# Delta-rule recurrence on one core: y computed by channel, its bank copied by ScalarE instead of transposed by VectorE

## The chip, the core and the metric

The kernel runs on one core of a Trainium2 chip (trn2). Its engines are TensorE (PE for matmuls, PEld for weight loads), VectorE (DVE), ScalarE (ACT), GpSimd (POOL) and SyncE (SP, which here issues DMAs). Each engine runs its own list of instructions in order and waits on semaphores. The metric is the device time of one launch, in microseconds, lower is better.

## The reference

A block with two halves: a delta-rule attention and a mixture of experts, each behind a modulated layer norm. Only the first half's recurrence is touched by the change. Cut to that:

```python
# B=4 sequences, T=1024 tokens, D=256, H=16 heads of DH=64; q, k, v: projection, causal conv of 4 taps, silu
k = k / jnp.maximum(jnp.linalg.norm(k, axis=-1, keepdims=True), 1e-12)
alpha, beta = jax.nn.sigmoid(h @ Wa.T + ba), jax.nn.sigmoid(h @ Wb.T + bb)      # per token and head
def step(S, xs):                                   # S: 64 x 64 for each sequence and head
    kt, vt, qt, at, bt = xs
    v_old = jnp.einsum('bhij,bhj->bhi', S, kt)
    upd = vt - at[..., None] * v_old
    S = jnp.clip(at * S + bt * upd[..., :, None] * kt[..., None, :], -5.0, 5.0)
    return S, jnp.einsum('bhij,bhj->bhi', S, qt)   # y of this token
y = ys * jax.nn.silu(h @ Wg.T + bg)
x = x + ga * (y @ Wo.T)                            # then the mixture of experts
```

## The kernel before

The recurrence is done in chunks of 64 tokens (`CW`), sixteen to a sequence. Tokens of one chunk are summed by matrix products, and only a 64 x 64 state `S` is carried from chunk to chunk. A **turn** is one pair of heads (`h` = 0, 1) of one pair of sequences (`b2` = 0, 1), so there are 16 turns (`TURNS`). Everything is laid out so that four 64 x 64 products, for the four (h, b2), sit in the four quarters of TensorE's array: the first operand and the moving one stand on 64 partitions (a row group), the output on 64 partitions of PSUM (a column group).

For chunk `c` the chain is: `seed_u` (L1613) and `state_into_u` (L1622) make `U` in PSUM from the state; ScalarE's `keep_u` (L731) copies it to SBUF; `state_sum` (L1633) makes the new part of the state; VectorE's `state` (L1052, L1049 for the first chunk) adds it to the part that ScalarE's `carry_state` (L742) has decayed. Then `seed_u` of the next chunk waits for that state (`s_st`).

The output y of two chunks, a pair `k` (0 to 7), is a sum of two products in one PSUM bank, `y_bank`: `y_of_state` (L1651), S times the decayed q (`qg`), and `y_of_u` (L1661), U times the masked matrix `A`. Two products of different row groups that add into the same PSUM cells are kept apart by the semaphore `s_yq`. After two pairs the bank is full (a quarter `q`, 0 to 3), VectorE's `turn_y` (L1058) transposes it in blocks of 32 from token-by-channel to channel-by-token into `yT`, and SyncE's `store_y` (L622) writes each half of a turn to DRAM with eight DMAs.

The order on every engine is written out by hand in one loop: iteration `it` interleaves, chunk by chunk, the chain of turn `it - 1` (`chain`, `tc`), the preparation of turn `it` (`prep`, `u`), the projection of k of turn `it + 1` (`new_k`, `un`), and the bound on the clipping of turn `it - 2` (`bound`, `tb`). Between the chain's steps TensorE does projections (L1386), transposes (L1507) and products of q and k (L1471). GpSimd's `solve` (L948 and L953, 31 rounds) inverts the triangular matrices of turn `u` from the end of `turn_matrix` (L1119, VectorE, end of an iteration) on; at chunk 13 VectorE's `rows_of_x` (L1183) and `turn_x` (L1177) wait for its last round, and also stand behind `state(tc, 13)` in VectorE's order. From there to the next `turn_matrix` runs the tail of an iteration. In the last chain iteration (`it` = 16) TensorE fills in with products of the gate (L122).

## Time and profile before

| | us |
|---|---|
| median of 3 runs | 1870.27 (1864.04 to 1873.93) |
| span of the profiled execution, first to last instruction | 1869.6 |
| the 15 iterations with a solve, `turn_matrix` of the first to that of the last | 55.5 to 1107.6 |
| chain of the last turn | 1171 to 1229 |
| the stages behind the recurrence | from 1248 |
| busy in the span: PE, DVE, POOL, ACT | 1620.9, 1389.8, 1127.0, 895.2 |

The own time of the profiled execution is not listed beside its span; the span lies 0.7 us under the median and inside the range of the three runs. An engine's busy time is a mean over stages; which engine holds up the recurrence has to be read from one iteration, engine by engine. In a timeline a row is a run of instructions of one line, with the start, the time to the last one's end, and in brackets the idle time of the engine before it. A matmul of fp32 leaves two records, so a group of 4 products reads x8.

### The profile page before, as it was taken

The page shows a single profiled execution, that of the slowest core. Times are in us where ns is not written, and L with a number is a line of the kernel's source. Part 1 is how long each engine was busy: PE and PEld are TensorE (multiplying, and loading weights), DVE is VectorE, ACT ScalarE, POOL GpSimd, SP SyncE. Part 2 cuts the span into 40 slices and gives each one's busy share as a digit, 9 for nine tenths or more (in the row PEclk, how much of TensorE's full clock was granted, in tenths as well). Part 3 has the DMA queues.
Part 4 walks back from the last instruction along what each step waited for, and adds up shares of the span by engine and source line. Part 5 has one row for each costly group of instructions (what it writes and reads, how often), then busy time and mean ns, then how long its engine had stood idle before and what let it go on. Part 6 is the DMA issues. An engine that isn't in the chain of part 4 may idle for free. (4 is left out here: it accounts for less than half of the span.)

```text
span 1869.6 us, 59680 instructions
## 1 busy us (share of the span) xinstructions
PE 1620.9 (87%) x24736; PEld 1142.6 (61%) x24736; DVE 1389.8 (74%) x1892; ACT 895.2 (48%) x1768; POOL 1127.0 (60%) x1362
## 2 busy tenths in 40 slices
PE   7778999999988989999988988835999848999997
PEld 4445666666666656566656666625888836666664
DVE  8777888888898888898898887447787664444443
ACT  5745555555655655655556555313444232222221
POOL 0657768768767767768777768017343103666664
PEclk9989989989999999989999988977999859999998
DMA  5221231231231231231231230246333163455543
GB/s 184 49 53 25 69 91 37 67 93 37 67 92 37 67 93 36 67 93 36 69 92 36 65 75 26 69 144 227 135 128 110 46 230 79 94 93 100 96 91 51
DMA packets 89465, 156.59 MB, mean 84 GB/s; under 512 B 15708, under 2 KB 54116, under 8 KB 88108
## 3 DMA queue, kind: packets, MB, share of 16 engines
q1 hardware_dynamic: 73292, 124.80, 22.6%
q0 software_dynamic: 15904, 27.93, 8.1%
q8 instruction: 202, 3.31, 0.8%
q14 instruction: 67, 0.55, 0.1%
HBM read 112.56 MB, written 40.12 MB: 82 GB/s over the span
## 5 line engine op out<-in xcount | busy, mean ns | idle before, releaser
L1386 PE MATMUL d_ps<-hT,turn_shared 128*128 128x512 f32 x768 | 402.8, 632 | 8.4 <-DVE d_Vp L1171 4.6
L953 POOL TENSOR_TENSOR turn_shared<-turn_shared,d_tmp 128x31 f32<-128x31 f32 (+15 forms) x496 | 289.7, 584 | 38.9
L948 POOL TENSOR_TENSOR d_tmp<-turn_shared 128x31 f32<-128x31 f32 (+15 forms) x496 | 286.4, 577 | 38.9
L1024 DVE SCALAR_TENSOR_TENSOR turn_shared<-d_ps,d_cw,turn_shared 128x1023 f32<-128x1023 f32 (+2 forms) x192 | 245.3, 1278 | 15.0 <-ACT turn_shared L682 12.6
L742 ACT ACTIVATE d_S<-d_S,gamma_chunk 128x64 f32<-128x64 f32 x448 | 130.9, 340 | 184.5 <-DVE d_S L1052 144.6
L2539 POOL DMA_INDIRECT m_xt<-rows_scratch,m_slot_i x71 | 70.2, 989 | 183.3 <-DVE m_slot_i L2632 95.7
L1386 PEld LDWEIGHTS d_ps<-hT,turn_shared 128*128 128x128 f32 x768 | 126.8, 192 | 87.6 <-issue 71.4
L2526 ACT ACTIVATE m_hm<-m_ps,m_b_tile 128x128 f32<-128x128 f32 x284 | 80.9, 368 | 206.3 <-PE m_ps L2706 206.3
L122 PE MATMUL o_po<-wo_split,y_high 128*128 128x256 f32 x512 | 101.7, 302 | 44.8 <-DVE y_low L115 44.8
L2549 POOL DMA_INDIRECT out<-m_yo,m_slot_i x71 | 114.2, 1608 | 41.2 <-issue 20.3
L2696 PE MATMUL m_ps<-m_w,m_xs 128*128 x284 | 136.2, 602 | 1.6 <-DVE m_xs L2641 1.0
L2287 POOL TENSOR_TENSOR y<-y,g_sb 128x512 f32<-128x512 f32 x48 | 78.8, 1676 | 94.7 <-ACT g_sb L2271 94.7
L2717 PE MATMUL m_ps<-m_w,m_hm 128*128 x568 | 134.4, 380 | 1.1 <-DVE m_yo L2658 1.1
L1651 PE MATMUL d_ps<-d_S,d_qg 64*64 64x64 f32 x1920 | 133.1, 241 | 1.1
L1024 DVE SCALAR_TENSOR_TENSOR d_v_made<-d_ps,d_cw,d_v_made 128x1023 f32<-128x1023 f32 (+2 forms) x96 | 122.3, 1274 | 14.0 <-ACT d_v_made L682 12.8
L731 ACT ACTIVATE d_U<-d_ps 128x128 f32<-128x128 f32 x256 | 70.0, 273 | 112.7 <-PE d_ps L1622 109.7
L1052 DVE TENSOR_TENSOR d_S<-d_S,d_ps 128x128 f32<-128x128 f32 x224 | 62.7, 280 | 80.8 <-PE d_ps L1633 70.5
L682 ACT ACTIVATE turn_shared<-d_ps,d_cw 128x1024 f32<-128x1024 f32 x64 | 77.0, 1203 | 94.2 <-PE d_ps L1386 93.5
L122 PEld LDWEIGHTS o_po<-wo_split,y_high 128*128 128x128 f32 x512 | 86.9, 208 | 47.2 <-issue 32.0
L1651 PEld LDWEIGHTS d_ps<-d_S,d_qg 64*64 64x64 f32 x1920 | 97.3, 144 | 26.0 <-issue 20.9
L2717 PEld LDWEIGHTS m_ps<-m_w,m_hm 128*128 128x128 f32 x568 | 102.4, 190 | 12.5 <-issue 1.5
L973 POOL MEMSET turn_shared<- 128x1024 f32 x16 | 15.2, 952 | 148.8 <-DVE turn_shared L1119 148.8
(251 smaller groups left out, 3737.2 us busy)
## 6 DMA issues: line engine op xcount, KB each, us to landing
turn_shared<-steps_scratch SPq DMA_DIRECT2D x64, 256.0 KB, 4.2
d_qg<-gamma_scratch SPq DMA_DIRECT2D x64, 256.0 KB, 5.0
y_scratch<-d_yT SPq DMA_DIRECT2D x256, 64.0 KB, 1.8
d_arow<-ab_scratch SPq DMA_DIRECT2D x128, 128.0 KB, 3.1
y<-y_scratch SPq DMA_DIRECT2D x8, 2048.0 KB, 8.7
m_w<-w_in SPq DMA_DIRECT2D x16, 512.0 KB, 10.0
turn_shared<-x_by_half_in SPq DMA_DIRECT2D x8, 512.0 KB, 6.8
rows_scratch<-gates SPq DMA_DIRECT2D x4, 1024.0 KB, 11.6
```

The costliest lines, as they stand in the source:

```text
L122: ins = nc.tensor.matmul(dst, lhs(a).bitcast(F32R), rhs(b).bitcast(F32R), start=first and n == 0, stop=last and n == 2)
L742: last = nc.scalar.activation(S[:, (c + 1) % SLOTS, b2, :], S[:, c % SLOTS, b2, :], ACT.Identity, scale=gC[:, b2, tc * NCW + c:tc * NCW + ...
L948: nc.gpsimd.tensor_tensor(tv, Tq[:, s + 1:, s].rearrange("p (r a) -> p r a", a=1).broadcast_to([P, left, known]), X[:, s, 0:known].rearran ...
L953: nc.gpsimd.tensor_tensor(X[:, s + 1:, 0:known], X[:, s + 1:, 0:known], tv, ALU.subtract).then_inc(s_sub, 1)
L1024: nc.vector.scalar_tensor_tensor(out=dst[:, j + 1:], in0=src[:, 0:T - 1 - j], scalar=cw[:, u // BP % 2, n, 2 - j:3 - j], in1=dst[:, j + 1: ...
L1386: return nc.tensor.matmul(dst[:, g, :], w[:, m % 2, n, dc, :], hT[:, dc, at:at + G], start=(dc == 0), stop=(dc == DC - 1))
L1651: last = nc.tensor.matmul(y_ps(c, h, b2), qg[rows64(h), tc % 2, b2, here(c)], S[rows64(h), c % SLOTS, b2, :].rearrange("p (j v) -> p j v", ...
L2287: nc.gpsimd.tensor_tensor(y[:, g % 2, m, :], y[:, g % 2, m, :], gate_kept[g][:, m, :] if g < EARLY else g_sb[:, i % 4, :], ALU.mult).then_ ...
L2526: last = nc.scalar.activation(hm[:, j % 2, f * P:(f + 1) * P], ps[:, 2, f * P:(f + 1) * P], ACT.Gelu, bias=b1_t[:, f, j:j + 1])
L2549: nc.gpsimd.indirect_dma_start(out, bass.IndirectOffsetOnAxis(ap=slot_i[:, j:j + 1], axis=0), yo[:, j % YRING, :], None, compute_op=ALU.ad ...
L2696: last = nc.tensor.matmul(ps[:, j % 2, :], xs[:, j % 2, dc * P:(dc + 1) * P], w1_s[:, bass.ds(e, 1), dc, :].rearrange("p a f -> p (a f)"), ...
L2717: last = nc.tensor.matmul(dst, hm[:, j % 2, f * P:(f + 1) * P], w2_s[:, bass.ds(e, 1), f, :].rearrange("p a d -> p (a d)"), start=f == 0, ...
```

## The change

The products of y change places: the state and U are now the first (stationary) operand and q and A the moving one, so that y comes out with the channel on the partition (head `h` in the rows, sequence `b2` in the columns). The bank then needs no transpose: ScalarE copies it as it is (`keep_y`), and VectorE's `turn_y` is gone. The two row groups are now those of `b2` in the products of U, and both add into the same cells, so `y_of_u` is parted in two calls, and the second waits on `s_yq` for the first; `y_of_state`, now with one row group for each column group, is one call where it was two. `store_y` writes with four DMAs, each of 128 partitions with two runs of 512 bytes, where it had eight of 32 partitions with two runs of 1024 bytes.

```diff
         def y_ps(c, h, b2):
-            return y_bank[rows64(b2), :].rearrange("p (h j t) -> p h j t", h=2, j=2)[:, h, :, c % 4 * CH:(c % 4 + 1) * CH]
+            return y_bank[rows64(h), :].rearrange("p (b j c t) -> p b j c t", b=2, j=2, c=4)[:, b2, :, c % 4, :]
...
                 sp.wait_ge(s_ye, 4 * t + 2 * q + 2)
-                for h, b2 in HEADS:
+                for b2 in range(2):
                     for s in range(2):
                         at = s * T // 2 + q * T // 4
-                        sp.dma_start(y_s[2 * (t % BP) + b2, t // BP][rows64(h), at:at + T // 4]
-                                     .rearrange("(j i) t -> i j t", j=2),
-                                     yT[quad(b2, s), h, :].rearrange("p (j t) -> p j t", j=2)).then_inc(s_yo, 16)
+                        sp.dma_start(y_s[2 * (t % BP) + b2, t // BP][:, at:at + T // 4].rearrange("p (q t) -> p q t", q=2),
+                                     yT[:, :, (2 * b2 + s) * P:(2 * b2 + s + 1) * P]).then_inc(s_yo, 16)
...
+            def keep_y(t, q):
+                act.wait_ge(s_y, HC * t + 2 * (q + 1))
+                if q % 2 == 0 and 2 * t + q // 2:
+                    act.wait_ge(s_yo, 64 * (2 * t + q // 2))
+                nc.scalar.activation(yT[:, q % 2, :], y_bank, ACT.Identity).then_inc(s_ye, 1)
...
-            def turn_y(t, q):
-                dve.wait_ge(s_y, HC * t + 2 * (q + 1))
-                if q % 2 == 0 and 2 * t + q // 2:
-                    dve.wait_ge(s_yo, 128 * (2 * t + q // 2))
-                nc.vector.transpose(flat(yT[:]).rearrange("p (a t) -> p a t", t=G // 2)[:, :, q % 2 * P:(q % 2 + 1) * P],
-                                    y_bank.rearrange("p (a t) -> p a t", t=P)).then_inc(s_ye, 1)
...
-            def y_of_state(tc, k, h):
...
+            def y_of_state(tc, k):
...
                 for c in ((1,) if k == 0 else (2 * k, 2 * k + 1)):
                     for b2 in range(2):
-                        last = nc.tensor.matmul(y_ps(c, h, b2), qg[rows64(h), tc % 2, b2, here(c)],
-                                                S[rows64(h), c % SLOTS, b2, :].rearrange("p (j v) -> p j v", j=2),
-                                                start=opens and (c == 1 or c % 2 == 0), stop=False)
+                        for h in range(2):
+                            last = nc.tensor.matmul(y_ps(c, h, b2), S[rows64(h), c % SLOTS, b2, :],
+                                                    qg[rows64(h), tc % 2, b2, here(c)].rearrange("p (j t) -> p j t", j=2),
+                                                    start=k % 2 == 0 and b2 == 0 and (c == 1 or c % 2 == 0), stop=False)
                 last.then_inc(s_yq, 1)
 
-            def y_of_u(tc, k):
-                pe.wait_ge(s_yq, 2 * (HC * tc + k) + 2)
-                pe.wait_ge(s_ue, NCW * tc + 2 * k + 2)
+            def y_of_u(tc, k, b2):
+                if b2 == 0:
+                    pe.wait_ge(s_yq, 2 * (HC * tc + k) + 1)
+                    pe.wait_ge(s_ue, NCW * tc + 2 * k + 2)
+                else:
+                    pe.wait_ge(s_yq, 2 * (HC * tc + k) + 2)
                 for c in (2 * k, 2 * k + 1):
-                    for h, b2 in HEADS:
-                        last = nc.tensor.matmul(y_ps(c, h, b2), A[rows64(b2), tc % 2, h, c, :],
-                                                U[rows64(b2), c % KEPT, h, :].rearrange("p (j v) -> p j v", j=2),
-                                                start=False, stop=c % 4 == 3 and h == 1)
-                last.then_inc(s_y, 1)
+                    for h in range(2):
+                        last = nc.tensor.matmul(y_ps(c, h, b2), U[rows64(b2), c % KEPT, h, :],
+                                                A[rows64(b2), tc % 2, h, c, :].rearrange("p (j t) -> p j t", j=2),
+                                                start=False, stop=c % 4 == 3 and b2 == 1)
+                last.then_inc(s_y if b2 else s_yq, 1)
```

`keep_y` stands in ScalarE's order behind `keep_u` and `carry_state` of chunks 4, 9 and 11 (quarters 0, 1, 2) and of chunk 0 of the next iteration (quarter 3), where `turn_y` stood in VectorE's. On TensorE every `y_of_u(tc, k)` becomes `y_of_u(tc, k, 0)` and `y_of_u(tc, k, 1)` one behind the other, in the old place. The joined `y_of_state` takes these places: for k = 1, 2 and 6 it stands whole between `seed_u` and the next `state_into_u` (chunks 2, 5, 12), where before only one half stood there and the other in chunk 3, 6 or 13; for k = 0 and 4 whole ahead of `seed_u` (chunks 1, 10), before one half on either side of it; for k = 3 whole behind `state_into_u` of chunk 8, before half of it behind the `seed_u` of that chunk; for k = 5 both halves stood together already (chunk 11); for k = 7 whole ahead of `w_product`.

TensorE's order at chunk 11 of the first iteration of the loop, before: the products of the state are L1651, those of U L1661, seeds L1613, `state_into_u` L1622, `state_sum` L1633.

```order
L1651 MATMUL d_ps<-d_S,d_qg 64x2x32 [waits d_state,d_y]
L1651 MATMUL d_ps<-d_S,d_qg 64x2x32 x3
L1651 MATMUL d_ps<-d_S,d_qg 64x2x32 [waits d_y_of_state]
L1651 MATMUL d_ps<-d_S,d_qg 64x2x32 x3
L1613 MATMUL d_ps<-d_Vp,gate_second 64x64 [waits d_state,d_u_kept]
L1613 MATMUL d_ps<-d_Vp,gate_second 64x64 x3
L1661 MATMUL d_ps<-d_U,d_A 64x2x32 [waits d_u_kept,d_y_of_state]
L1661 MATMUL d_ps<-d_U,d_A 64x2x32 x7
```

The same place of the changed kernel, where the lines are L1650, L1663 and L1615:

```order
L1650 MATMUL d_ps<-d_qg,d_S 64x2x32 [waits d_state,d_y]
L1650 MATMUL d_ps<-d_qg,d_S 64x2x32 x7
L1615 MATMUL d_ps<-d_Vp,gate_second 64x64 [waits d_state,d_u_kept]
L1615 MATMUL d_ps<-d_Vp,gate_second 64x64 x3
L1663 MATMUL d_ps<-d_A,d_U 64x2x32 [waits d_u_kept,d_y_of_state]
L1663 MATMUL d_ps<-d_A,d_U 64x2x32 x3
L1663 MATMUL d_ps<-d_A,d_U 64x2x32 [waits d_y_of_state]
L1663 MATMUL d_ps<-d_A,d_U 64x2x32 x3
```

The number of products is the same; the wait on `d_y_of_state` between two halves has moved from the products of the state to those of U.

ScalarE's order at chunks 4 to 5 of the changed kernel; before, the row L802 is not there, and the others follow one another:

```order
L733 ACTIVATE d_U<-d_ps 128x128 [waits d_u]
L744 ACTIVATE d_S<-d_S,gamma_chunk 128x64 [waits d_state]
L744 ACTIVATE d_S<-d_S,gamma_chunk 128x64
L802 ACTIVATE d_yT<-d_ps 128x512 [waits d_y]
L733 ACTIVATE d_U<-d_ps 128x128 [waits d_u]
L788 ACTIVATE d_ktok<-d_ps 128x1024 [waits d_k_turned]
```

The copy of the bank now stands ahead of the next `keep_u` (L733, before L731).

## Rows read from the trace of the kernel before

**Rows 1.** First lines of the page: span, busy time of each engine.

```profile
span 1869.6 us, 59680 instructions
...
PE 1620.9 (87%) x24736; PEld 1142.6 (61%) x24736; DVE 1389.8 (74%) x1892; ACT 895.2 (48%) x1768; POOL 1127.0 (60%) x1362
```

**Rows 2.** Windows: stretch in us, busy of PE, PEld, DVE, ACT, POOL, clock, DMA.

```profile
413.00:458.00 45.00, 43.50 (x741) 27.32 (x741) 39.47 (x52) 25.77 (x54) 39.28 (x66) 1.00 0.20 49
458.00:480.00 22.00, 17.72 (x546) 13.27 (x542) 20.64 (x21) 14.66 (x21) 13.42 (x7) 0.84 0.26 76
1171.20:1229.00 57.80, 53.65 (x791) 38.23 (x792) 27.88 (x51) 21.95 (x59) 3.86 (x2) 0.94 0.19 53
```

**Rows 3.** One line's instructions, L1119: duration ns, first and last start.

```profile
L1119 DVE STREAM_TRANSPOSE turn_shared<-turn_shared x16: 1945/1973/1989, 55.5 to 1107.6; 128x1024 f32<-128x1024 f32 x16
```

**Rows 4.** Timeline of VectorE, one turn: start, us, idle before and its releaser.

```profile
416.29 0.29 DVE L1052 TENSOR_TENSOR d_S<-d_S,d_ps 128x128 f32<-128x128 f32 x1 [0.84 <-PE d_ps L1633]
...
457.82 0.29 DVE L1052 TENSOR_TENSOR d_S<-d_S,d_ps 128x128 f32<-128x128 f32 x1 [1.00 <-PE d_ps L1633]
458.03 2.09 DVE L1183 STREAM_TRANSPOSE turn_shared<-turn_shared 128x1024 f32<-128x1024 f32 x1
...
479.82 1.96 DVE L1119 STREAM_TRANSPOSE turn_shared<-turn_shared 128x1024 f32<-128x1024 f32 x1
```

**Rows 5.** Timeline of GpSimd in the same turn.

```profile
457.76 0.24 POOL L953 TENSOR_TENSOR turn_shared<-turn_shared,d_tmp 128x31 f32<-128x31 f32 x1
```

**Rows 6.** Timeline of all engines near 736 us, four turns later.

```profile
735.67 0.24 POOL L953 TENSOR_TENSOR turn_shared<-turn_shared,d_tmp 128x31 f32<-128x31 f32 x1
...
737.64 2.09 DVE L1183 STREAM_TRANSPOSE turn_shared<-turn_shared 128x1024 f32<-128x1024 f32 x1
```

**Rows 7.** Timeline of TensorE (PE) in the turn of rows 4.

```profile
419.72 0.68 PE L1661 MATMUL d_ps<-d_U,d_A 64*64 64x64 f32 x16
420.45 0.34 PE L1633 MATMUL d_ps<-d_U,gate_second 64*64 64x64 f32 x8
...
424.36 0.38 PE L1613 MATMUL d_ps<-d_Vp,gate_second 64*64 64x64 f32 x5
...
424.88 0.34 PE L1622 MATMUL d_ps<-d_S,d_WT 64*64 64x64 f32 x8
...
430.08 0.68 PE L1661 MATMUL d_ps<-d_U,d_A 64*64 64x64 f32 x16
430.77 0.45 PE L1613 MATMUL d_ps<-d_Vp,gate_second 64*64 64x64 f32 x8
...
435.58 0.45 PE L1651 MATMUL d_ps<-d_S,d_qg 64*64 64x64 f32 x8
436.25 0.34 PE L1633 MATMUL d_ps<-d_U,gate_second 64*64 64x64 f32 x8 [0.22 <-ACT d_U L731]
...
451.24 0.68 PE L1661 MATMUL d_ps<-d_U,d_A 64*64 64x64 f32 x16
451.70 0.34 PE L1633 MATMUL d_ps<-d_U,gate_second 64*64 64x64 f32 x8
451.99 0.85 PE L1651 MATMUL d_ps<-d_S,d_qg 64*64 64x64 f32 x12
...
452.67 0.28 PE L1651 MATMUL d_ps<-d_S,d_qg 64*64 64x64 f32 x4
```

**Rows 8.** Waits over the span: total us, times, longest us.

```profile
ACT d_U L731 <- PE d_ps L1622: 109.7, 136, 3.7
...
PEld d_ps L1651 <- PE d_ps L1651: 3.3, 16, 0.2
```

**Rows 9.** Groups by line: busy us, mean ns, idle before.

```profile
L1058 DVE STREAM_TRANSPOSE d_yT<-d_ps 128x512 f32<-128x512 f32 x64 | 45.6, 713 | 10.5 <-PE d_ps L1661 5.4 <-DMA y_scratch<-d_yT 4.6
...
L2278 ACT ACTIVATE o_rows<-o_pb 128x512 f32<-128x512 f32 x16 | 9.5, 596 | 105.3 <-PE o_pb L2410 105.3
```

**Rows 10.** DMA issues: count, KB each, median us to landing.

```profile
y_scratch<-d_yT SPq DMA_DIRECT2D x256, 64.0 KB, 1.8
```

More of the change, by code:

```diff
@@ L873, in _ @@
                         keep_w(tc, 1)
+                    if bound and c == 0:
+                        keep_y(tb, 3)
                     if prep and c == 1:
@@ L892, in _ @@
                         carry_state(tc, 5)
+                    if chain and c == 4:
+                        keep_y(tc, 0)
                     if prep and c == 5:
@@ L909, in _ @@
                         carry_state(tc, 10)
+                    if chain and c == 9:
+                        keep_y(tc, 1)
                     if new_k and c == 10:
@@ L914, in _ @@
                         carry_state(tc, 12)
+                    if chain and c == 11:
+                        keep_y(tc, 2)
                     if chain and c == 12:
@@ L1292, in _ @@
                         scalars(u)
-                    if bound and c == 0:
-                        turn_y(tb, 3)
                     if prep and c == 1:
@@ L1327, in _ @@
                         bound_max(tb, 0)
-                    if chain and c == 9:
-                        turn_y(tc, 1)
                     if new_k and c == 9:
@@ L1339, in _ @@
                         tap_k(un, 0, 1)
-                    if chain and c == 11:
-                        turn_y(tc, 2)
                     if new_k and c == 12:
@@ L1781, in _ @@
                         proj_v(u, 1, 3)
-                    if chain and c == 6:
-                        y_of_state(tc, 2, 1)
                     if chain and c == 7:
-                        y_of_u(tc, 2)
+                        y_of_u(tc, 2, 0)
+                        y_of_u(tc, 2, 1)
                     if chain and c == 8:
-                        y_of_state(tc, 3, 0)
+                        y_of_state(tc, 3)
                     if new_k and c == 9:
@@ L1792, in _ @@
                     if chain and c == 11:
-                        y_of_u(tc, 4)
+                        y_of_u(tc, 4, 0)
+                        y_of_u(tc, 4, 1)
                     if new_k and c == 12:
                         proj_k(un, 1, 0)
-                    if chain and c == 13:
-                        y_of_state(tc, 6, 1)
                     if new_k and c == 14:
@@ L1841, in _ @@
                         seed_u(tc, 4)
-                        y_of_state(tc, 1, 1)
                     if chain and c == 4:
-                        y_of_u(tc, 1)
+                        y_of_u(tc, 1, 0)
+                        y_of_u(tc, 1, 1)
                         seed_u(tc, 5)
@@ L1866, in _ @@
                         seed_u(tc, 9)
-                        y_of_state(tc, 3, 1)
                     if chain and c == 9:
-                        y_of_u(tc, 3)
+                        y_of_u(tc, 3, 0)
+                        y_of_u(tc, 3, 1)
                         seed_u(tc, 10)
```

59 lines of the change are left out of this document (28 added, 31 removed).

## The prediction

> **What bounds the kernel now.** The page first: PE is busy for 87% of the span, VectorE for 74%, ScalarE for 48% [rows 1]. The change takes work from VectorE and gives it to ScalarE, so the question is which engine holds up an iteration of the recurrence. `turn_matrix` starts from 55.5 to 1107.6 us, fifteen intervals, so an iteration takes 70.1 us [rows 3]. I took the one from 411.1 to 479.8 us, the shortest kind, and cut it at the moment where `rows_of_x` starts, 458.03. In the first stretch, 413 to 458, PE is busy for 43.50 of 45.00 us, VectorE for 39.47, ScalarE for 25.77. In the second, the tail, VectorE is busy for 20.64 of 22.00 us and PE for only 17.72 [rows 2]. So the tail is VectorE's, 21.8 us from `rows_of_x` to the next `turn_matrix` [rows 4]. None of the four transposes of y stands in it: three stand ahead of chunk 13 and one in chunk 0, behind `turn_matrix`.
>
> What sets the start of the tail? Two things, and they meet. GpSimd's last round ends at 457.76 + 0.24 = 458.00 [rows 5], and `rows_of_x` starts at 458.03. But VectorE's own last step ahead of it, `state(13)`, ran from 457.82 to 458.11 and had waited 1.00 us for PE's `state_sum` [rows 4]; also at chunk 1 VectorE waited 0.84 us for PE [rows 4]. So in the first stretch VectorE has room, PE has none, and GpSimd's solve is level with PE. In other iterations, as at 736 us, GpSimd is done at 735.91 and `rows_of_x` starts at 737.64 [rows 6]: there PE's chain is 1.7 us late and GpSimd has room.
>
> That gives the rule for the sum: what VectorE saves ahead of chunk 13 buys little, and what PE's order loses there is added to every iteration, since GpSimd's room in the short iterations is nil and in the long ones is used up already.
>
> **VectorE's part.** The 64 transposes cost 713 ns each, 45.6 us in all, and 10.5 us of waiting ahead of them [rows 9]: 2.85 us busy in each turn. Bounds: 0 (all of it ahead of chunk 13 goes into VectorE's waits for PE, which grow) and 45.6 us (VectorE sets everything). I take 0, because of the 1.00 and 0.84 us of waiting. If PE's cover were gone, these 2.85 us would be the gain of a turn.
>
> **ScalarE's part.** It gets 64 copies of 128x512 from PSUM. The nearest row is a copy of that shape, 596 ns [rows 9], so 38 us in all, 2.4 us for each turn. Behind each copy the next `keep_u` is queued, and PE's `state_sum` waits for that. `keep_u` waited for PE in 136 cases, 109.7 us, so 0.8 us at a time [rows 8]; that is the room that hides a copy of 0.6 us. I take 0, with 2.4 us a turn as the other end. The copy frees the bank about as early as the transpose did, and PE did not wait for the bank before.
>
> **The store.** Eight DMAs, 1.8 us from issue to landing each [rows 10], become four of twice the size. VectorE waited 4.6 us in all for these landings [rows 9]; ScalarE's `keep_y` of chunk 11 would wait instead. Fewer issues on SyncE's queue should make the last one land no later. I take 0, and 4.6 us as its upper bound.
>
> **PE's part: the waits.** The number of products is the same, and so is their pace: eight records of `y_of_state`, which share a row group, take 0.45 us, and sixteen of `y_of_u`, on the diagonal, 0.68 us [rows 7], so from the first start to the last 0.23 and 0.46 us, if the last record takes 0.22. Where a half waits for the other, the price is seen at chunk 11, the one place where both halves of `y_of_state` stood together (the profile counts 16 such waits [rows 8]): from 451.99 to 452.67 + 0.28 = 452.95, so 0.96 us where sixteen records without a wait take 0.68 [rows 7]. A wait costs 0.28 us. After the change there are eight such waits in a turn (one in each `y_of_u`) and that of chunk 11 is gone.
>
> How many are covered? In chunk 2 `y_of_u` starts at 419.72 and `state_sum` at 420.45, 0.73 us later where 0.46 are needed; in chunk 4 `seed_u` starts 0.69 us after it [rows 7]. Such places (k = 0, 1, 2, 3) have 0.23 to 0.27 us of room, because the next group waits for ScalarE or VectorE: 0.05 us is left of each, 0.2 together. The one at k = 6 stands behind `state_sum(13)` and is in the tail. In chunk 11 `state_sum` follows `y_of_u` by 0.46 us (451.24, 451.70): no room, full price, and so for k = 5 and for k = 7 in chunk 0. That is 3 x 0.28 - 0.28 (the wait that is gone) + 0.2 = 0.76 us.
>
> **PE's part: the places.** `state_into_u` waits until `seed_u` has finished: in chunk 2 seeds start at 424.36, and `state_into_u` at 424.88, 0.52 us later, the length of a group of eight (0.45, as at 430.77) and the semaphore [rows 7]. The half of `y_of_state` behind the seed hides in that. A second half doesn't fit, so it adds 0.23 us in chunks 2, 5 and 12. What it leaves gives nothing back: in chunk 6 that half ran at 435.58 in time in which `state_sum`, at 436.25, waited for ScalarE [rows 7]. In chunk 10 the half that hid behind the seed moves ahead of it, again about 0.2 us. Sum 0.9 us. Bounds for this term: 0, if the order of the records fills the gap after all, and 0.9.
>
> **The sum.** 0.76 + 0.9 = 1.66, and I take 1.6 us, since in chunk 6 `keep_u` is held by ScalarE's own work and takes up some of it. Fourteen iterations at 1.6, and 1.3 for the first, which has no k = 7: 23.7 us. In the last chain PE is busy for 53.65 of 57.80 us [rows 2]; seven more waits at 0.28 make 2.0 us, hidden nowhere but in chunk 0: I take 1.5. Together 25.2 us on the span of 1869.6 [rows 1]: 1894.8. The span stands 0.7 us under the median of the runs shown: about 1895 us, 1.3% slower.
>
> The Trainium skill ("TensorE: Matmul & The Clock Gate", section "Single matmul latency") puts the fixed part of a warm matmul's latency at 398 cycles of 2.4 GHz, 166 ns. A wait for one's own product would cost about that, an estimate from that page. This trace has 0.28 us, semaphore and refill included; by the page's figure the eight waits would cost 0.11 us less each, and the kernel would come out near 1890 us.
>
> **Rivals.**
> 1. VectorE sets the iteration, faster. Its place is VectorE's order ahead of chunk 13; each transpose taken away moves `state` and the taps behind it forward. For it: VectorE is busy for 39.47 of 45 us there, and in iterations such as that of 736 us the tail starts late, behind a transpose. Against it: the 1.00 us wait for PE. Full price 45.6 us less, 1825 us; but GpSimd's solve allows only the lateness, 1.7 us in perhaps half of the iterations, about 12 us: 1858 us. It decides if PE's extra waits stay below 0.5 us a turn. Chance 0.16.
> 2. Covered on both sides, no change: PE's waits fall into times in which it waits anyway, as the gaps of 0.2 us at `state_sum` suggest, and the late iterations give back what the short ones lose. 1865 to 1875 us. Chance 0.15.
> 3. ScalarE's copies delay `keep_u` as well: 0.6 us, four times a turn, fully exposed would be 38 us more, 1933 us; at half of it 1914 us. For it: they stand ahead of `keep_u` in the chain. Against it: the 0.8 us of waiting. Chance 0.12.
> 4. The forecast, PE's waits and places alone: 1882 to 1907 us. Chance 0.57.
>
> **How the numbers follow.** A change of 0.5%, 9.4 us, is about what a measurement of this kernel can tell from none. Slower by more than that: cases 3 and 4 but for a small part of case 4 near its lower end, 0.67. Same: case 2 and that part, 0.17. Faster: case 1, 0.16. The likeliest case gives 1895 us. The range, 1862 to 1913 us, leaves out most of case 1 and the upper half of case 3.
>
> **What the profile after would show.** `turn_y` gone and VectorE's busy time down by 45 us; ScalarE's up by 38 us. About 128 waits of the second `y_of_u` for the first, with 0.28 us between the groups beyond the usual pace. An iteration of 71.6 us in place of 70.1, with a tail that is still 21.8 us; `rows_of_x` about 1.6 us behind GpSimd's last round in every iteration, and VectorE's wait for PE ahead of `state(13)` grown from 1.0 to about 2.5 us. `keep_u` must still wait for PE behind a `keep_y`, not the other way round. I would be wrong if `rows_of_x` starts with GpSimd's last round in all iterations (then PE had room that I don't see), if the tail gets shorter, or if ScalarE is what PE waits for in chunks 1, 5, 10 and 12.

## The result: 6.3 us slower, a quarter of what was forecast

| | before | after |
|---|---|---|
| median of 10 runs each, us | 1868.10 (1864.04 to 1873.93) | 1874.35 (1868.66 to 1880.19) |
| ratio, 95% interval | | 1.0035 (1.0019 to 1.0052) |
| span of the profiled execution, us | 1869.6 | 1872.4 |
| `turn_matrix`, first to last | 55.5 to 1107.6 | 55.8 to 1110.0 |
| an undisturbed iteration | 68.72 | 69.61 |

The profiled execution of the changed kernel took 1873.98 us. Its page, first lines:

```profile
span 1872.4 us, 59552 instructions
...
PE 1615.0 (86%) x24736; PEld 1124.6 (60%) x24736; DVE 1354.9 (72%) x1828; ACT 925.0 (49%) x1832; POOL 1127.0 (60%) x1362
```

Against [rows 1]: VectorE's busy time fell by 34.9 us, where 45 were expected, and ScalarE's rose by 29.8, where 38 were. The durations of all VectorE's instructions sum to 40.8 us less (`turn_y` is gone with 45.6, some others take a little longer), and since records of one engine overlap in time, the busy time falls by less than that. Windows of one undisturbed iteration and of the last chain (stretch, busy of PE, PEld, DVE, ACT, POOL, granted clock, DMA share, GB/s):

```profile
830.00:876.00 46.00, 43.91 (x734) 26.99 (x734) 37.88 (x48) 27.65 (x58) 40.09 (x66) 1.00 0.27 71
876.00:898.00 22.00, 17.97 (x548) 13.46 (x546) 20.63 (x21) 14.63 (x21) 12.47 (x7) 0.84 0.23 69
1174.00:1230.00 56.00, 51.16 (x758) 35.29 (x758) 21.10 (x41) 21.95 (x59) 2.84 (x2) 0.94 0.16 50
```

The columns answer to [rows 2]: PE is still the engine without room ahead of the tail, and VectorE is at 37.88 of 46 us. The line of `turn_matrix`, now L1128, answers to [rows 3]:

```profile
L1128 DVE STREAM_TRANSPOSE turn_shared<-turn_shared x16: 1950/1973/1986, 55.8 to 1110.0; 128x1024 f32<-128x1024 f32 x16
```

The intervals sum to 1054.2 us, 2.1 more than before, so 70.28 for 70.14. That small difference hides two large ones. Here is VectorE at both ends of one undisturbed iteration (828.29 to 897.90, so 69.61 us), and behind it GpSimd's last round in it:

```profile
828.29 1.97 DVE L1128 STREAM_TRANSPOSE turn_shared<-turn_shared 128x1024 f32<-128x1024 f32 x1
...
875.88 0.29 DVE L1068 TENSOR_TENSOR d_S<-d_S,d_ps 128x128 f32<-128x128 f32 x1 [1.29 <-PE d_ps L1635]
876.09 2.09 DVE L1192 STREAM_TRANSPOSE turn_shared<-turn_shared 128x1024 f32<-128x1024 f32 x1
...
897.90 1.98 DVE L1128 STREAM_TRANSPOSE turn_shared<-turn_shared 128x1024 f32<-128x1024 f32 x1
```

```profile
874.80 0.24 POOL L969 TENSOR_TENSOR turn_shared<-turn_shared,d_tmp 128x31 f32<-128x31 f32 x1
```

GpSimd is done at 875.04 and `rows_of_x` (L1192) starts at 876.09, 1.05 us late, where it was 0.03 us late in [rows 4, 5]. VectorE's wait for PE ahead of `state(13)` is 1.29 us, where it was 1.00. The tail is 21.8 us, as before. So PE now sets every iteration, as forecast, but by 1.05 us, and an undisturbed iteration got longer by 0.89 us, where the prediction had 1.6. In this profile fewer iterations are disturbed, too. The waits (total us, times, longest):

```profile
DVE d_S L1068 <- PE d_ps L1635: 113.0, 102, 3.6
...
ACT d_U L733 <- PE d_ps L1624: 89.2, 99, 4.2
...
PEld d_ps L1663 <- PE d_ps L1663: 25.7, 128, 0.3
...
ACT d_yT L802 <- PE d_ps L1663: 19.3, 32, 1.6
```

`keep_u` still waits for PE behind the copies; `keep_y` (L802) waited for PE alone, never for a DMA.

### The profile page after: what moved, and what is told of

Same layout as the page of the kernel before. It is cut to its first block and busy times, and to the rows that moved or that the text cites. A ratio compares the mean times of both kernels' runs of the same rounds, so it can differ in the third digit from the quotient of the medians.

```text
span 1872.4 us, 59552 instructions
## 1 busy us (share of the span) xinstructions
PE 1615.0 (86%) x24736; PEld 1124.6 (60%) x24736; DVE 1354.9 (72%) x1828; ACT 925.0 (49%) x1832; POOL 1127.0 (60%) x1362
## 3 DMA queue, kind: packets, MB, share of 16 engines
q1 hardware_dynamic: 87628, 124.79, 21.8%
## 5 line engine op out<-in xcount | busy, mean ns | idle before, releaser
L969 POOL TENSOR_TENSOR turn_shared<-turn_shared,d_tmp 128x31 f32<-128x31 f32 (+15 forms) x496 | 296.5, 598 | 38.9
L964 POOL TENSOR_TENSOR d_tmp<-turn_shared 128x31 f32<-128x31 f32 (+15 forms) x496 | 279.9, 564 | 38.9
L1663 PE MATMUL d_ps<-d_A,d_U 64*64 64x64 f32 x2048 | 113.8, 227 | 8.4 <-issue 0.2
L733 ACT ACTIVATE d_U<-d_ps 128x128 f32<-128x128 f32 x256 | 70.0, 274 | 90.3 <-PE d_ps L1624 89.2
L1473 PE MATMUL d_ps<-turn_shared 64*64 64x64 f32 x4096 | 77.6, 226 | 27.1 <-DVE beta_turned L1100 12.2
## 6 DMA issues: line engine op xcount, KB each, us to landing
rows_scratch<-gates SPq DMA_DIRECT2D x4, 1024.0 KB, 13.1
```

The source lines that it names most:

```text
L964: nc.gpsimd.tensor_tensor(tv, Tq[:, s + 1:, s].rearrange("p (r a) -> p r a", a=1).broadcast_to([P, left, known]), X[:, s, 0:known].rearran ...
L969: nc.gpsimd.tensor_tensor(X[:, s + 1:, 0:known], X[:, s + 1:, 0:known], tv, ALU.subtract).then_inc(s_sub, 1)
L1663: last = nc.tensor.matmul(y_ps(c, h, b2), U[rows64(b2), c % KEPT, h, :], A[rows64(b2), tc % 2, h, c, :].rearrange("p (j t) -> p j t", j=2) ...
```

## The experiments

The differences are against the kernel before, timed beside it on the same chip, by medians. "Undisturbed" is the interval between two `turn_matrix` in an iteration in which TensorE has no stop (what that is comes below): the value that most such iterations of the profile share.

| kernel | median, us | before beside it | difference | ratio to before, 95% | undisturbed iteration |
|---|---|---|---|---|---|
| changed kernel | 1874.35 | 1868.10 | +6.3 | 1.0035 (1.0019 to 1.0052) | 69.61 |
| 6 changed kernel, timed again | 1875.89 | 1868.28 | +7.6 | 1.0034 (1.0020 to 1.0048) | 69.62 |
| 1 old places | 1867.53 | 1867.45 | +0.1 | 1.0010 (0.9994 to 1.0027) | 69.23 |
| 2 VectorE copies | 1878.22 | 1867.45 | +10.8 | 1.0051 (1.0032 to 1.0071) | 69.70 |
| 3 waits, by sequence | 1936.60 | 1867.45 | +69.2 | 1.0385 (1.0360 to 1.0410) | 73.2 |
| 4 halves about the seeds | 1863.26 | 1867.45 | -4.2 | 0.9980 (0.9964 to 0.9995) | 69.21 |
| 7 waits, by head | 1884.26 | 1868.28 | +16.0 | 1.0066 (1.0044 to 1.0087) | 69.66 |
| 8 last pair about the seed | 1861.37 | 1868.28 | -6.9 | 0.9962 (0.9947 to 0.9976) | 69.04 |
| 11 the same, in the changed kernel | 1874.61 | 1870.31 | +4.3 | 1.0021 (1.0003 to 1.0038) | 69.43 |
| 13 before, code moved by 64 | 1872.64 | 1869.19 | +3.5 | 1.0028 (1.0012 to 1.0044) | 68.73 |
| 14 changed, code moved by 64 | 1879.76 | 1869.19 | +10.6 | 1.0059 (1.0038 to 1.0079) | 69.62 |
| 9 before, code moved by 128 | 1868.34 | 1870.31 | -2.0 | 0.9989 (0.9970 to 1.0007) | 68.73 |
| 10 changed, code moved by 128 | 1882.71 | 1870.31 | +12.4 | 1.0074 (1.0045 to 1.0104) | 69.62 |
| 12 kernel 8, code moved by 128 | 1870.16 | 1870.31 | -0.2 | 1.0008 (0.9988 to 1.0028) | 69.05 |
| 15 before, code moved by 192 | 1874.71 | 1869.19 | +5.5 | 1.0037 (1.0019 to 1.0056) | 68.72 |
| 16 changed, code moved by 192 | 1883.06 | 1869.19 | +13.9 | 1.0087 (1.0067 to 1.0106) | 69.62 |
| 17 before, gamma rows late | 1862.39 | 1868.60 | -6.2 | 0.9971 (0.9952 to 0.9990) | 68.73 |
| 18 changed, gamma rows early | 1879.16 | 1868.60 | +10.6 | 1.0058 (1.0035 to 1.0081) | 69.62 |

### The terms of the sum: kernels 1, 2, 4, 8, 11

Kernel 1 takes back the joining of `y_of_state`:

```diff
-            def y_of_state(tc, k):
+            def y_of_state(tc, k, b2):
...
                     if chain and c == 5:
                         seed_u(tc, 6)
-                        y_of_state(tc, 2)
+                        y_of_state(tc, 2, 0)
...
+                    if chain and c == 6:
+                        y_of_state(tc, 2, 1)
```

> The changed kernel with y_of_state parted by sequence and its halves at the old places (no wait between them), so that only the waits inside y_of_u are left of what the change adds to TensorE's order. Theory A (read from the two traces: places worth about 0.55 us of an undisturbed iteration, waits 0.3): iteration of the recurrence 69.6 -> 69.1 us, 8 us less than the changed kernel, about 1866 us. Theory B (the prediction's sizes: places 0.9, waits 0.76, and VectorE's saved time gives 0.8 back): 13 us less, 1861 us. Theory C (places cost nothing, all is waits): as the changed kernel, 1874 us.

Measured: 6 to 7.5 us less than the changed kernel, and 0.38 us of an undisturbed iteration. The prediction's 0.9 us for the places was more than twice the measured price. Chunk by chunk (starts of `state_into_u` and `state_sum` from `turn_matrix` on, changed kernel less before): the place in chunk 2 costs 0.19 us by chunk 3, of which 0.17 come back in chunk 4, where `state_sum` waits for ScalarE less (0.31 us for 0.48); that in chunk 5 costs 0.08, given back in chunk 6; those in chunks 10 and 12 cost 0.24 and 0.18.

Kernel 2 gives the copies to VectorE, at the old places of `turn_y`:

```diff
-                    if chain and c == 4:
-                        keep_y(tc, 0)
...
                     if chain and c == 4:
+                        copy_y(tc, 0)
                         update_max(tc, 0)
```

> The changed kernel, but VectorE copies the bank, at the places where it transposed it before; ScalarE does not. TensorE's order is that of the changed kernel. It tells what relieving VectorE gave. Theory A (VectorE's time ahead of chunk 13 is nearly all waiting for TensorE, and ScalarE's copies cost nothing): 0 to 5 us more than the changed kernel, 1874 to 1879 us. Theory B (the relief gave back 0.8 us of the 1.66 us that TensorE lost in each iteration): 12 us more, 1886 us. Theory D (ScalarE's copies delayed keep_u and cost something themselves): less than the changed kernel.

Measured: 3 to 4.5 us above the changed kernel, 0.09 us of an undisturbed iteration. VectorE's relief was worth about this, and ScalarE's copies cost nothing that taking them away would give back. The kernel does both at once, so the 0.09 us are their sum; but chunk by chunk ahead of the tail no `state_into_u` or `state_sum` starts earlier than in the changed kernel. The prediction's two zeros were right.

Kernel 4 is kernel 1 with the second half of `y_of_u` behind the seed that follows, for k = 1, 3, 6, 7:

```diff
                     if chain and c == 4:
                         y_of_u(tc, 1, 0)
-                        y_of_u(tc, 1, 1)
                         seed_u(tc, 5)
+                        y_of_u(tc, 1, 1)
```

> The version with the old places, and in addition the second half of y_of_u stands behind the seed that follows it (k = 1, 3, 6; for k = 7 the seed of chunk 1 stands between the halves), so that the seed runs in the time of the wait. Theory A: iteration 68.7 to 68.8 us, where GpSimd's rounds set it; 11 to 13 us less than the changed kernel, 1861 to 1863 us, unless TensorE's stops of about 1 us come back (13 us in the trace of before, 3 in that of after). Theory B: 1.7 us less for each iteration than the changed kernel is not to be had, since GpSimd holds the iteration at 68.7: the same 1861. Theory E (moving halves apart costs as much as it hides): as the version with the old places alone.

The iteration got shorter by 0.02 us only (that the time fell by 4.3 us against kernel 1 all the same, no run here explains). For k = 7 the move gives 0.17 us (`state_sum` of chunk 1 starts within 0.01 us of where it did before the change), and for k = 1 it loses 0.19: there the seed waits for the state anyway, and the second half had its place ahead of it. So kernel 8 moves k = 7 alone:

```diff
+                    if bound and c == 0:
+                        y_of_u(tb, 7, 0)
                     if chain and c == 0:
                         seed_u(tc, 1)
                     if bound and c == 0:
-                        y_of_u(tb, 7, 0)
                         y_of_u(tb, 7, 1)
```

> The version with the old places, and only the last pair's second half of y_of_u (k = 7, chunk 0) behind the seed of chunk 1; k = 1, 3, 6 as in the changed kernel. Theory A (the wait in chunk 0 costs 0.2 us, moving k = 1 behind its seed costs 0.23, the rest is one or the other alike): an undisturbed iteration of 68.97 us, where the two versions before had 69.23 and 69.21; 4 us less than the version with the old places, about 1863 us. Theory E (nothing to be had): 1867 us.

69.04 us against 68.97 expected, and 1861.4 us: the parts add up. In the changed kernel itself the same move is worth 0.18 us of an iteration:

> The changed kernel, in which only the order of three calls in chunk 0 differs: first half of y_of_u of the last pair, seed of chunk 1, second half. y_of_state stays at the changed kernel's places. Theory A (the parts add up: this move was worth 0.20 us with the old places): an undisturbed iteration of 69.4 us where the changed kernel has 69.6; 3 us less, about 1872 us. Theory E (what is won in chunk 0 is lost at the places of chunks 2 and 5): 1874 to 1875 us.

### What a wait costs: kernels 3 and 7

Both put a wait between two halves of `y_of_u` into the kernel before, kernel 3 by sequence as in the change, kernel 7 by head:

```diff
-                for c in (2 * k, 2 * k + 1):
-                    for h, b2 in HEADS:
+                for b2 in range(2):
+                    for c in (2 * k, 2 * k + 1):
...
+                    if b2 == 0:
+                        last.then_inc(s_yq, 1)
+                        pe.wait_ge(s_yq, 3 * (HC * tc + k) + 3)
```

> The kernel before, in which y_of_u is parted by sequence and the second half waits for the first, as in the change; all else, with VectorE's transposes and the places of y_of_state, as before. Theory A: 0.3 us for each iteration, 4 to 5 us more than before, about 1873 us. Theory B (the prediction's 0.76 us and the one more at chunk 11 that is not taken away here, 1.04): 11 to 16 us more, 1879 to 1884 us. Theory C (the waits are hidden): as before, 1868 us.

It was 69 us slower, which no theory had. TensorE in kernel 3:

```profile
440.05 0.34 PE L1633 MATMUL d_ps<-d_U,gate_second 64*64 64x64 f32 x8 [0.48 <-ACT d_U L731]
440.19 1.20 PE L1662 MATMUL d_ps<-d_U,d_A 64*64 64x64 f32 x13
```

The first eight records of L1662 started over 0.43 us, where eight records of `y_of_u` in the changed kernel take 0.23. In the layout before, the products of one sequence all stand on one quarter of the array. Over the whole run the median of a half was 0.456 us from first to last start on one quarter, and 0.230 us on two. The experiment had changed the pace as well as the wait, so it says nothing on the wait. Kernel 7 parts by head, which keeps two quarters in turn:

> The kernel before with a wait between the halves of y_of_u, parted by head this time, so that each half still alternates between two quarters of the array (eight records in 0.23 us, where the halves by sequence stood on one quarter and took 0.46). Theory A: waits cost 0.5 us for each iteration (as the version with the old places shows: 69.23 against 68.72 us), 7 us more than before, 1875 us. Theory B (the prediction's 0.28 us for each wait that has no room, 1.04 us with that of chunk 11 kept): 15 us more, 1883 us. Theory H (what the first experiment on waits lost came from the waits, not from the one quarter): 60 us more.

Theory B, the prediction's own price, was right here: 16.0 us where 15 were expected, 0.94 us of an undisturbed iteration where 1.04 were. TensorE at chunk 11 of the kernel before, of kernel 7, and of the changed kernel (two views of it, the second closer):

```profile
870.05 0.34 PE L1622 MATMUL d_ps<-d_S,d_WT 64*64 64x64 f32 x8
870.33 0.68 PE L1661 MATMUL d_ps<-d_U,d_A 64*64 64x64 f32 x16
870.79 0.34 PE L1633 MATMUL d_ps<-d_U,gate_second 64*64 64x64 f32 x8
...
872.52 0.27 PE L1622 MATMUL d_ps<-d_S,d_WT 64*64 64x64 f32 x1
```

```profile
877.00 0.34 PE L1622 MATMUL d_ps<-d_S,d_WT 64*64 64x64 f32 x8
877.28 0.90 PE L1662 MATMUL d_ps<-d_U,d_A 64*64 64x64 f32 x13
877.97 0.27 PE L1633 MATMUL d_ps<-d_U,gate_second 64*64 64x64 f32 x1
...
878.31 0.85 PE L1651 MATMUL d_ps<-d_S,d_qg 64*64 64x64 f32 x12
...
879.34 0.90 PE L1662 MATMUL d_ps<-d_U,d_A 64*64 64x64 f32 x13
880.03 0.27 PE L1622 MATMUL d_ps<-d_S,d_WT 64*64 64x64 f32 x1
```

```profile
868.73 0.34 PE L1624 MATMUL d_ps<-d_S,d_WT 64*64 64x64 f32 x8
868.89 0.79 PE L1663 MATMUL d_ps<-d_A,d_U 64*64 64x64 f32 x11
...
869.88 0.68 PE L1650 MATMUL d_ps<-d_qg,d_S 64*64 64x64 f32 x16
870.42 0.41 PE L1615 MATMUL d_ps<-d_Vp,gate_second 64*64 64x64 f32 x7
...
870.68 0.80 PE L1663 MATMUL d_ps<-d_A,d_U 64*64 64x64 f32 x11
```

```profile
869.47 0.27 PE L1635 MATMUL d_ps<-d_U,gate_second 64*64 64x64 f32 x1
```

From `state_into_u` (L1622, L1624) to `state_sum` (L1633, L1635) kernel 7 takes 0.97 us and the changed kernel 0.74; before it was 0.74 as well ([rows 7] show its second part, 0.46 from `y_of_u` on). The gap itself is alike in both: the second half starts 0.28 us behind the last record of the first (medians over the 128 groups: 0.285 us in kernel 7, 0.278 in the changed kernel). But in kernel 7 and before, `y_of_u` starts 0.28 us behind `state_into_u`, in the changed kernel 0.16, and its first eight records take 0.19 us there for 0.23. What the first half gains so pays for most of the gap. So a wait has the price that the prediction gave it, 0.28 us, but at k = 4 the changed kernel pays nothing for it. From `state_sum` to the next `state_into_u`, with k = 5 between, kernel 7 takes 2.06 us and the changed kernel 1.80, before 1.73: 0.33 us for the wait in the old layout, 0.07 in the changed kernel, where the wait in `y_of_state` is gone as well. Kernel 1, with the new layout and the old places, has 0.78 and 1.88 us here, so it pays 0.04 and 0.15. At k = 7 all three pay the same, 0.18 to 0.19.

### Where the rest went: stops for code

Undisturbed, an iteration is 0.89 us longer, and the last chain 2.4 us (from the first `state` to the last, 50.5 before, 52.9 after). 15 x 0.89 + 2.4 = 15.8 us, but 6.3 and 7.6 were measured. The two traces also differ in something that neither the diff nor the prediction names. TensorE in iteration 4 of the kernel before:

```profile
342.97 1.13 PE L1386 MATMUL d_ps<-hT,turn_shared 128*128 128x512 f32 x2
344.03 0.27 PE L1633 MATMUL d_ps<-d_U,d_ktok 64*64 64x64 f32 x1
345.81 0.34 PE L1633 MATMUL d_ps<-d_U,d_ktok 64*64 64x64 f32 x7 [1.52 <-issue]
```

For 1.52 us it stands in the middle of a group, and the row says "issue": nothing it waits for is late. I count such stops of 0.3 us or more, where no semaphore stands between the products on either side. Ahead of the tail the first profile of before has seven, 8.0 us together, and that of the changed kernel three, 2.4 us. `rows_of_x`, summed over the fifteen iterations, stands 13.3 us further behind GpSimd's last round before and 2.8 us after than it would in undisturbed iterations; that sum holds all lateness, not the stops alone. The thirteen stops of the kernel before that lie between 127 and 1230 us have one thing in common: 1.3 to 1.6 us ahead of each stop's end a 16 KB packet of the DMA queue "instruction" has landed. The reading is that TensorE waits for its own program; the row of a packet doesn't name an engine, and the kernels with moved code test it.

Kernel 5 (kernel before, unchanged, one profile) and kernel 6 (changed kernel, unchanged):

> The kernel before, unchanged, profiled in another execution. In the first profile TensorE stops seven times by 0.8 to 1.5 us between the chunks ahead of the tail, with nothing late that it waits for, 13 us in all. Each of these stops ends 1.2 to 1.5 us after a 16 KB packet of the DMA queue named instruction has landed. Theory F (the stops sit where the blocks of TensorE's code begin, so that they come back): at least five of the seven at the same chunk of the same iteration. Theory G (each execution draws its own): other places, another sum.

> The changed kernel, unchanged, profiled and timed again. Its first profile has three such stops ahead of the tail, 2.4 us in all. Theory F: the same three, at 157, 578 and 928 us. Theory G: others. The time again about 1874 us, 6 us more than before.

Four of seven came back before (5.0 us into iteration 4, 30.5 into 7, 3.4 into 9, 3.5 into 15), with other lengths; this execution took 1859.7 us. (The 13 us in the text above are the lateness of `rows_of_x`, not the sum of the seven stops.) In the changed kernel one of three did (7), and three in the tails. The places recur, the lengths vary, so both theories are half right. The 128 waits that the next kernels add ahead of TensorE's first product move its code and change neither a product nor the order:

```diff
+            for _ in range(128):
+                pe.wait_ge(s_c, 16)
             pe.wait_ge(s_wm, 32)
```

> The kernel before with 128 more semaphore waits, all long met, ahead of TensorE's first product, where it waits for its first loads anyway. No product and no order changes; TensorE's code from there on lies 128 instructions further. Theory F (the stops of 0.3 to 1.5 us, each ending 1.2 to 1.5 us after a 16 KB packet of the instruction queue has landed, sit where a block of TensorE's code ends): in the two profiles of before four stops are at the same chunks (5.0 us into iteration 4, 30.5 into 7, 3.4 into 9, 3.5 into 15), here those places are free of stops and others have them. The sum of the stops may be less or more than 4 to 8 us ahead of the tail, and the time moves by up to 10 us either way. Theory G (the stops come from the work that goes on at those places, whatever the code's position): the same four places, the same time, 1868 us.

> The changed kernel with the same 128 waits ahead of TensorE's first product. Theory F: its stops (65.6 us into iteration 2, 66.4 into 3, 66 into 8, which both profiles have) go elsewhere; the undisturbed iteration stays 69.61 us. If the changed kernel had fewer stops than before by its code's position alone, then with both kernels moved the difference between them is another than 6 to 7 us, up to the 13 us that its longer iteration is worth (0.89 us, fifteen times). Theory G: the same places, 1874 us.

> The fastest version so far (old places, last pair's second half behind the seed, 1861 us) with the same 128 waits ahead of TensorE's first product. Theory F: other places of the stops, the undisturbed iteration of 69.04 us as before; the time within 5 us of 1861. Theory K (its lead of 7 us over the kernel before is owed to the position of its code, since its undisturbed iteration is 0.3 us longer than that of before): the lead is gone or halved against the kernel before that is moved as well.

The old places are free of stops, and others have them (3.0 us into iteration 4, 3.6 into 5, 29.9 into 8, 3.7 into 11, 30.5 into 14 among them). In kernel 10, too, the places of the changed kernel are free and others have stops (30.1 us into iteration 2, 65.8 into 4, 30.2 into 8, 30.3 into 14). Theory F holds. Kernel 12 is the sobering one: the lead of kernel 8 over the kernel before, 6.9 us, is gone once its code lies 128 instructions further: 1870.16 us, 1.8 above kernel 9. And the moved pair differs by 14.4 us. Part of that is ahead of the recurrence: iteration 1 begins at 130.2 us in kernel 10 and at 126.4 in kernel 9. Two more positions:

> The kernel before with 64 semaphore waits, long met, ahead of TensorE's first product. Theory F (position of the code): undisturbed iteration 68.72 us, stops at other places than with 0 and 128 waits; the time anywhere from 1860 to 1876 us. Theory G (position is nothing): 1868 to 1870 us.

> The changed kernel with 64 such waits. Theory L (the order's own price is 0.89 us for each iteration, 13 us, and 6 to 7 us is the lucky position): 11 to 20 us more than the kernel before that is moved alike. Theory M (the pair at 128 is the odd one, the price is 6 us): 3 to 9 us more.

> The kernel before with 192 such waits; the first product starts 1 to 3 us later than unmoved, which is the same in both kernels. Theory F: undisturbed iteration 68.72 us, again other places of the stops, 1862 to 1879 us.

> The changed kernel with 192 such waits. Theory L: 11 to 20 us more than the kernel before that is moved alike. Theory M: 3 to 9 us more. The undisturbed iteration stays 69.61 us by either.

The differences, changed less before, are 6.3 and 7.6 (unmoved, measured twice), 7.1, 14.4 and 8.4 us; the mean over the four positions is 9.2. Theory L expected 11 to 20 and fails at 64 and 192; so luck of position isn't the main thing. Only kernels moved alike are compared here, for the added waits also hold up the start: the first product comes at 8.3 us unmoved and at 8.5, 9.6 and 13.1 us with 64, 128 and 192 waits, the same to 0.1 us in both kernels (for 192, 1 to 3 us later were expected, and it was 4.7), so that much of kernel 15's +5.5 us is not the position. In the profiles the fifteen iterations together exceed fifteen undisturbed ones by 9.4 to 21.3 us in the five of the kernel before (mean 16.4), and by 6.2 to 18.6 us in the five of the changed kernel (mean 11.1). That is 5.3 us less, and 15.8 less 5.3 is 10.5 us, near the 9.2 measured; the spread shows how little one pair of profiles says. What is systematic shows when the stops are sorted by place. Between 3 and 7 us into an iteration the five profiles of the kernel before (unmoved twice, then 64, 128 and 192) have 4, 3, 1, 4 and 3 stops, 2.4 to 5.3 us in a profile; the five of the changed kernel have none. (One of the four at 128, 0.41 us, stands at a met semaphore; it ends 1.5 us behind a packet of code like the rest.)

### The wait that moved: kernels 17 and 18

Why there? The gamma rows, four transfers of 256 KB into `qg` for the next turn, are issued by SyncE. It waits in `gamma_rows` for `s_yq`, which before the change was complete with `y_of_state` of the last pair, in the tail. The change counts the first half of `y_of_u` on the same semaphore, and for the last pair that half stands in chunk 0 of the next iteration. SyncE's issues, the kernel before and the changed one, iteration 4 (`turn_matrix` at 339.3 and 337.6):

```profile
336.70 2.37 SPq L615 DMA_DIRECT2D d_qg<-gamma_scratch  x4
```

```profile
341.00 2.37 SPq L615 DMA_DIRECT2D d_qg<-gamma_scratch  x4
```

They went from 2.6 us ahead of `turn_matrix` to 3.4 us behind it. And this is what they had been in the way of (queue, kind: packets, MB, share of 16 engines), first in the kernel before from 336 to 343 and from 343 to 345 us, then in the changed kernel from 336 to 340:

```profile
q1 hardware_dynamic: 728, 1.64, 86.1%
```

```profile
q1 hardware_dynamic: 89, 0.07, 16.7%
q8 instruction: 1, 0.02, 3.5%
```

```profile
q1 hardware_dynamic: 257, 0.31, 21.5%
q8 instruction: 1, 0.02, 1.5%
```

Before, data takes 86% of the DMA engines for seven microseconds, and the window lists no packet of code; one is loaded at 343.4, and TensorE goes on 2.4 us later. In the changed kernel the packet comes at 338.4, 0.8 us into the iteration. This is no single case: over the fifteen iterations the first packet of code behind `turn_matrix` starts at a median of 3.8 us in the kernel before and at 1.4 in the changed one. The last two kernels swap this one wait and nothing else:

```diff
-                    sp.wait_ge(s_yq, 2 * HC * (u - 1))
+                    sp.wait_ge(s_y, HC * (u - 1))
```

in the kernel before (kernel 17, gamma rows late), and in the changed one (kernel 18, gamma rows early)

```diff
-                    sp.wait_ge(s_yq, 2 * HC * (u - 1))
+                    sp.wait_ge(s_yq, 2 * HC * (u - 1) - 1)
```

> The kernel before, in which the load of the gamma rows waits for y_of_u of the last pair where it waited for y_of_state of it. Nothing else changes. Theory N (these four transfers hold up the block of code that TensorE needs in chunks 0 and 1, and the changed kernel has them out of the way by accident): the loads are issued 3 to 4 us behind turn_matrix, the block of code is loaded 1 to 2 us behind it, the stops between 3 and 7 us are gone, and the time is 4 to 8 us less than before, 1860 to 1864 us. Theory O (the load's place is nothing): 1868 us.

> The changed kernel, in which the load of the gamma rows waits for y_of_state of the last pair alone, as it did before the change. Theory N: the loads are issued 3 us ahead of turn_matrix, stops of 0.4 to 1.5 us come back between 3 and 7 us of three or four iterations, and the time is 4 to 8 us more than the changed kernel, 1879 to 1883 us, 11 to 15 more than before. Theory O: 1875 us.

Both moved the way theory N said: kernel 17 to 6.2 us less than before (ratio 0.9971, 0.9952 to 0.9990), kernel 18 to 3.0 to 4.3 us more than the changed kernel had over before, a little under the 4 to 8 of the theory. The first is clear of its interval; the second is not by itself, as the intervals of kernel 18 and of the changed kernel overlap, but the packets and the stops in its trace moved as the theory says: the median start of the first packet is 1.6 us in kernel 17 and 3.5 in kernel 18. The whole of its fifteen iterations shows no loss, though: they exceed undisturbed ones by 7.6 us, in the changed kernel by 10.0 and 11.4. So in the new order the 3 to 4 us rest on the medians alone. SyncE and TensorE in iteration 4 of kernel 17 (`turn_matrix` at 333.3), where the group that was cut is whole:

```profile
336.97 3.30 SPq L615 DMA_DIRECT2D d_qg<-gamma_scratch  x4
```

```profile
342.67 0.35 PE L1633 MATMUL d_ps<-d_U,d_ktok 64*64 64x64 f32 x8
```

and of kernel 18 (`turn_matrix` at 335.4), where it is cut again:

```profile
332.81 2.37 SPq L615 DMA_DIRECT2D d_qg<-gamma_scratch  x4
```

```profile
340.40 0.27 PE L1635 MATMUL d_ps<-d_U,d_ktok 64*64 64x64 f32 x1
341.64 0.34 PE L1635 MATMUL d_ps<-d_U,d_ktok 64*64 64x64 f32 x7 [0.98 <-issue]
```

Between 3 and 7 us kernel 17 has no stop and kernel 18 has three, in iterations 4, 10 and 15.

So the order of TensorE costs 10.6 us with the gamma rows early in both (kernel 18 against before), and 12 to 14 with them late in both (+6.3 or +7.6 for the changed kernel, less the -6.2 of kernel 17). The moved load gives back 3 to 6 of it, surely in the old order and likely in the new. Two other engines wait for the same semaphore, ScalarE's `carry_state` and VectorE's `state` of chunk 0; in the changed kernel's profile these waits come to one of 0.8 us.

## Why the prediction was wrong, by its own steps

1. **What bounds the kernel.** Right. PE's chain ahead of chunk 13 sets the start of the tail, the tail kept its 21.8 us, and a loss of PE is added to every iteration. The late chain that it saw at 736 us [rows 6] stood in iteration 9, one of those with stops for code.
2. **VectorE's part, 0.** Right: 0.09 us of an undisturbed iteration, 3 to 4.5 us in all (kernel 2), of a bound of 45.6.
3. **ScalarE's part and the store, 0.** Right. `keep_u` waited for PE 89.2 us in all where it had waited 109.7 [rows 8]: the copies went into that room. The four larger stores took 3.1 us from issue to landing where the eight had taken 1.8, but nothing waited for them.
4. **PE's waits, 0.76 us.** The price of one, 0.28 us, held; kernel 7 bore out the whole step within 0.1 us in the layout in which it was measured. The smaller price, by the 166 ns of the Trainium skill ("TensorE: Matmul & The Clock Gate", section "Single matmul latency"), did not hold. Carried over to the new layout it was too much: kernel 1, which has all these waits and the old places, is 0.51 us above before. It charged 0.28 us each at k = 4, 5 and 7 less 0.28 for the wait that went; k = 7 cost 0.18, and k = 4 and 5 with that wait gone cost 0.07 together in the changed kernel and 0.19 in kernel 1. The prediction counted the room behind a group and not what the first half gains when it starts closer behind the group ahead.
5. **PE's places, 0.9 us.** Mis-sized: 0.38 us. "What it leaves gives nothing back" was false in chunk 4, where ScalarE held `state_sum` and 0.17 us came back, and chunk 5's, 0.08 us where 0.23 were charged, came back in chunk 6. Only chunks 10 and 12 paid.
6. **The sum.** 1.6 us for an iteration was 0.89; the last chain's 1.5 us was 2.4.
7. **The step that is missing.** The prediction asked where waits stand on TensorE and never who else waits for `s_yq`. The diff shows that `y_of_u` now counts on it; SyncE's `gamma_rows` does not stand in the diff. Its four transfers left the place where they had kept TensorE's code away, which gave back 6.2 us in the old order (kernel 17) and by the medians 3 to 4.3 in the new (kernel 18). No rival had this. Rival 2, no change, had the number (1865 to 1875) with another reason.

With steps 4 and 5 at their measured sizes the forecast would have been 15 x 0.89 + 2.4 = 15.8 us, and 10 to 13 us with the moved load's share taken off: within the 6.3 to 14.4 us of the four positions of the code, whose mean is 9.2. The rest, 2 to 5 us between 15.8 and the 10.6 to 14 of the order alone, I can't assign: iterations with a stop are partly late already, but no run shows it by itself, and the intervals of these differences are some 4 us wide on either side.

## What to carry to other kernels

When a change adds to a semaphore or moves what counts on it, list every waiter on every queue, also those that the diff doesn't touch, and ask what each one issues. Price a wait in the layout in which it will stand: what its neighbours can overlap decides more than the wait itself. And where a long unrolled program is timed to half a percent, move the code by a few dozen instructions and take it again before believing a lead; kernel 8's 6.9 us did not outlive that.

## What the chip showed that I had not expected

The program arrives in packets of 16 KB, 202 of them in the profiled execution on a queue of their own (the rows don't say for which engine), and some arrive late for TensorE: from the first `turn_matrix` on the stops of the recurrence sum to 14.7 us in the first profile of before and to 11.0 in the second. That is 3.7 of the 11.4 us by which the spans of these two differ, and kernels 17 and 18 show that part of the stops depends on other DMA traffic. The Trainium skill ("Runtime: NRT & Kernel Launch", section "Instruction fetch mechanics") says that code is fetched in blocks of 16 KB while earlier ones run, and that the cost of a boundary is mostly hidden. The trace agrees on the size and on "mostly", but the exceptions cost 0.3 to 2.8 us each here, and with four transfers of 256 KB in flight they came in chunks 0 and 1 of up to four iterations in a profile.

Four products of 64 x 64 on one quarter of the array took 0.46 us from first to last start, on two quarters in turn 0.23. The Trainium skill ("TensorEngine Tiling (Array Packing)", section "Key Properties") says that tiles work independently of each other. The trace agrees in that a group spread over two quarters starts in half the time; kernels 3 and 7, which part `y_of_u` by sequence (one quarter) or by head (two) and are alike otherwise, differ by 53 us.
